# Who issues the quantiser's weight transfers inside attention: ScalarE, or SyncE at the end of its steps

## The reference, cut to what matters

```
h = layernorm(x) * (1 + ca) + sa
x = x + ga * attention(h)                      # rope, causal softmax, 4 query heads share a key/value head
h = layernorm(x) * (1 + cb) + sb
x = x + gb * ffn(h)

ternary_quant(w): w = bf16(w); in groups of 64:
    scale = max(mean(|w|), 1e-8);  q = clip(round(w / scale), -1, 1);  w + (q * scale - w)
ffn: gate, up = split(h @ quant(w_gate_up).T);  a = silu(gate) * up;  rms_norm(a) @ quant(w_proj).T
```

## Time and profile before

| | |
|---|---|
| time, median of 3 runs | 1734.54 us (1732.52 to 1736.47) |
| the profiled execution | 1730.82 us, span of its instructions 1729.0 us |
| TensorE busy | 1675.4 us (97%) |
| VectorE busy | 1248.8 us (72%) |
| ScalarE busy | 1140.5 us (66%) |
| GpSimd busy | 977.1 us (57%) |
| TensorE's granted clock, mean | 0.994 of full speed |
| SyncE's transfers (queue q1) | 140.99 MB, 28.7% of the 16 transfer engines' time |
| ScalarE's transfers (queue q10) | 48.25 MB, 10.2% |

### The profile page before, as it was taken

One profiled execution on the slowest core, in us unless ns is written; L12 is line 12 of the kernel. 1 busy time (PEld: TensorE's weight loads), 2 busy tenths in 40 slices (PEclk: granted clock), 3 DMA queues, 4 the chain that ended last, 5 costly groups with the idle time before them and its releaser, 6 DMA issues. The chain is left out here.

```text
span 1729.0 us, 27586 instructions
## 1 busy us (share of the span) xinstructions
PE 1675.4 (97%) x8993; PEld 1386.7 (80%) x8993; DVE 1248.8 (72%) x2518; ACT 1140.5 (66%) x2315; POOL 977.1 (57%) x822
## 2 busy tenths in 40 slices
PE   6899999999999999999999999889999899999998
PEld 2588888888888888888888888667788688888886
DVE  6788889888889888888888988873333564545433
ACT  4588888888888888888888888863232443323222
POOL 1367777777777777777677777445000245444453
PEclk9999999999999999999999999999999999999999
DMA  7234444445445354454354454456555101001000
GB/s 295 71 106 118 131 122 124 122 112 137 112 117 142 99 132 126 103 139 128 96 148 114 107 132 126 132 152 203 188 187 173 53 1 31 25 13 43 0 31 25
DMA packets 174969, 190.92 MB, mean 110 GB/s; under 512 B 31456, under 2 KB 117736, under 8 KB 174832
## 3 DMA queue, kind: packets, MB, share of 16 engines
q1 hardware_dynamic: 137840, 140.99, 28.7%
q10 hardware_dynamic: 36992, 48.25, 10.2%
HBM read 86.12 MB, written 31.74 MB: 68 GB/s over the span
## 5 line engine op out<-in xcount | busy, mean ns | idle before, releaser
L1102 DVE TENSOR_TENSOR p_lo<-ps_b,p_hi 128x512 fp32r<-128x512 f32 x576 | 395.1, 688 | 103.3 <-ACT p_hi L987 99.5
L987 ACT CAST p_hi<-ps_b 128x512 fp32r<-128x512 f32 x576 | 338.2, 589 | 116.3 <-PE ps_b L889 87.7
L1002 ACT ACTIVATE p<-ps_b,negm 128x640 f32<-128x640 f32 (+7 forms) x512 | 382.9, 752 | 41.2 <-DVE negm L1113 39.8
L1113 DVE CUSTOM_DVE_ANT_0 ps_b<-ps_b,mask_w 128x640 f32<-128x640 f32 (+7 forms) x512 | 385.4, 760 | 21.6 <-PE ps_b L878 17.6
L889 PE MATMUL ps_b<-ident,p 128*128 128x128 f32 x2304 | 345.6, 274 | 9.2 <-DVE p_lo L1102 9.1
L889 PEld LDWEIGHTS ps_b<-ident,p 128*128 128x128 f32 x2304 | 271.9, 140 | 56.1 <-DVE p_lo L1102 13.4
L877 PE MATMUL ps_b<-k_hh,q_hl 128*128 128x512 f32 (+3 forms) x768 | 265.6, 347 | 7.5 <-ACT p L1002 6.8
L903 PE MATMUL ps_b<-p_hi,v_hl 128*128 128x512 f32 x576 | 257.9, 448 | 4.0 <-ACT o_sb L995 3.5
L878 PE MATMUL ps_b<-k_l,q_hl 128*128 128x512 f32 (+3 forms) x768 | 256.2, 347 | 0.0
L904 PE MATMUL ps_b<-p_lo,v_hl 128*128 128x512 f32 x576 | 226.6, 393 | 0.0
L1741 PE MATMUL ps_d<-h_hi,gu 128*128 128x512 f32 x512 | 200.6, 392 | 2.4 <-DVE h_lo L1861 2.4
(11 more groups left out here) (160 smaller groups left out, 3123.6 us busy)
## 6 DMA issues: line engine op xcount, KB each, us to landing
rot_x<-rot_s SPq DMA_DIRECT2D x320, 64.0 KB, 2.0
q_hl<-rot_s SPq DMA_DIRECT2D x128, 128.0 KB, 2.6
q_hl<-rot_x SPq DMA_DIRECT2D x128, 128.0 KB, 2.8
rd_all<-reciprocals SPq DMA_DIRECT2D x128, 128.0 KB, 3.0
o_low<-o_sb ACTq DMA_DIRECT2D x128, 128.0 KB, 2.3
attention_out<-o_sb SPq DMA_DIRECT2D x128, 128.0 KB, 2.5
o_raw<-attention_out SPq DMA_DIRECT2D x32, 512.0 KB, 4.7
wf<-in_L_ffn_w_gate_up ACTq DMA_DIRECT2D x28, 256.0 KB, 3.1
```

The costliest lines, as they stand in the source:

```text
L987: act.copy(p_hi[:, T % P_RING, :], ps[:, T_BANK + T % 2, :]).then_inc(phi_ready, 1)
L1002: act.activation(p_32[:, parity, h, column * P:column * P + nk], s, ACT.Exp, bias=negm[:, k:k + 1], scale=-1.0, accum_out=den[:, parity, k ...
L1102: dve.tensor_tensor(p_lo[:, T % P_RING, :], ps[:, T_BANK + T % 2, :], p_hi[:, T % P_RING, :].bitcast(F32), ALU.subtract).then_inc(plo_read ...
L1113: dve.tensor_tensor_reduce(s, s, mask_w[:, S - nk:S], 1.0, HIGHEST, ALU.add, ALU.min, negm[:, k:k + 1]).then_inc(max_ready, 1)
```

## The change

The two kinds of transfer are issued by SyncE instead of ScalarE, in the same steps, at places 350 and 360, behind everything else that SyncE issues in a step. The functions take the engine as an argument and stand ahead of all engines' programs, so that the output projection can still call them for ScalarE. Waits and semaphores are the same.

```
-UNIT_STORES = Places(own_units(15), 620)
-UNIT_LOADS = Places(own_units(0), 630)
+UNIT_STORES = Places(own_units(15), 350)
+UNIT_LOADS = Places(own_units(0), 360)
...
+        def store_unit(eng, g, u):
+            to = unit_of(g, u, tern_gu_g, tern_p_g)
+            units_tern.await_(eng, g, u)
+            eng.dma_start(to, unit_tile(u, w_hat)).then_inc(tern_out, 16)
+
+        def unit_load(eng, g, u):
+            units_sign.await_(eng, g, u - 1)
+            eng.dma_start(unit_tile(u, unit_raw(g, u)), unit_of(g, u, gu_g, wp_g)).then_inc(wf_in, 16)
...
         # SyncE's step, behind the O_LOAD part and ahead of WEIGHT_LOADS in the text
+                for g, u in body.units(T, at, UNIT_STORES):
+                    store_unit(sp, g, u)
+                for g, u in body.units(T, at, UNIT_LOADS):
+                    unit_load(sp, g, u)
-            bodies(step, SWAPS, PLACINGS, SAVES, SPREADS, STORES, WEIGHT_LOADS)
+            bodies(step, SWAPS, PLACINGS, SAVES, SPREADS, STORES, WEIGHT_LOADS, UNIT_STORES, UNIT_LOADS)
...
         # ScalarE's step
-                for g, u in body.units(T, at, UNIT_STORES):
-                    store_unit(g, u)
-                for g, u in body.units(T, at, UNIT_LOADS):
-                    unit_load(g, u)
...
-            outputs.scalar(act, unit_load, unit_parts, store_unit)
+            outputs.scalar(act, lambda g, u: unit_load(act, g, u), unit_parts, lambda g, u: store_unit(act, g, u))
```

More of the change, by code:

```diff
@@ L717, in unit_tile, with unit_raw @@
             return tile[:] if u >= 2 else tile[:].rearrange("p (r h) -> p r h", r=2)
+        gu_g = w_gu.rearrange("(g u p) d -> g u p d", g=KVH, p=P)
+        wp_g = w_p.rearrange("(u r p) (g h) -> g u p r h", u=2, p=P, g=KVH)
+        tern_gu_g = tern_gu.rearrange("(g u p) d -> g u p d", g=KVH, p=P)
+        tern_p_g = tern_p.rearrange("(u r p) (g h) -> g u p r h", u=2, p=P, g=KVH)
+        def unit_raw(g, u):
+            return places.wf_late if g == KVH - 1 and u >= LAST_UNITS else wf
+        def store_unit(eng, g, u):
[5 more added lines that the diff above has]
+            eng.dma_start(unit_tile(u, unit_raw(g, u)), unit_of(g, u, gu_g, wp_g)).then_inc(wf_in, 16)
         def quarters(ap, kind):
@@ L952, in _ @@
         def _(act):
[L953 to L956, removed]
             def shift(g, n):
@@ L960, in shift @@
                 act.dma_start(o_low[:, n % 2, :], o_sb[D:P, n % 2, :]).then_inc(o_shifted[n % 2], 16)
[L962 to L972, removed]
             def unit_abs(g, u):
@@ L1082, in step @@
                     unit_sign(g, u)
-                for g, u in body.units(T, at, UNIT_STORES):
-                    store_unit(g, u)
-                for g, u in body.units(T, at, UNIT_LOADS):
-                    unit_load(g, u)
             bodies(step, KEY_SCALES, ROUNDINGS, VALUE_ROWS, VALUE_HIGHS, HIGHS, COPIES, SHIFTS, EXPONENTIALS, KEY_HIGHS, QUERY_HIGHS,
-                   UNIT_ABS, UNIT_SIGNS, UNIT_STORES, UNIT_LOADS)
+                   UNIT_ABS, UNIT_SIGNS)
             def unit_parts(g, u):
```

## The result

The changed kernel took 1750.80 us (median of 4 runs, 1749.59 to 1752.01) against 1733.53 us before in the same sessions: ratio 1.0099, 95% interval 1.0084 to 1.0115. It is slower by about 17 us, 2 us more than the 1748.5 that were predicted, and inside the range. A second session with the same kernel gave 1.0084 (1.0066 to 1.0103).

A forecast was written before the change was run, and what follows sets the result against it. TensorE was taken to bound seven of eight head groups, busy 937.4 of 940 us. Losses of 7 x (1.17 + 0.77) = 13.6 us take 1730.82 to 1744.5, or 1748.5 on the median; 8-in-10 range 1738 to 1759.

The forecast's parts named there:

- ScalarE's relief is worth nothing: Removing 88 issues, some 32 us, from ScalarE's queue gains between 0 and 2.6 us on the path, taken as 0.
- Four of the six units are early enough, and the stores too: Loads at SyncE's step end come early enough for four units; the tightest store keeps 2.2 us before VectorE's pick.
- Units 2 and 5 come 1.79 and 2.31 us ahead of Abs: Behind SyncE's other transfers, these loads start a mean 1.79 and 2.31 us before ScalarE's Abs, over seven groups.
- Landing 3.16 and 3.51 us, from the spreads at that place: Loads of units 2 and 5 take the mean times of SyncE's spreads issued there, 3.16 and 3.51 us.
- Waits of 1.37 and 1.20 us: ScalarE's Abs waits for its load 1.37 us at unit 2 and 1.20 us at unit 5, each once a group.
- The slack of TensorE, 0.2 and 0.43 us: Slack behind Abs: some 0.2 us at unit 2; at unit 5 0.19 us ScalarE idle plus 0.24 us before the scores.
- The place where it shows: TensorE loses 1.17 us behind unit 2's block copy and 0.77 us behind unit 5's exponential, idle at steps 28 and 63.
- The sum of 13.6 us: TensorE's loss over seven groups, 7 x (1.17 + 0.77) = 13.6 us, with the last group unchanged.
- The ring order: On SyncE's ring the load would queue behind the placing's transfers, landing nearer to 3.5 us; spreads and loads don't part this.

The follow-up runs named there:

- Both early: Changed kernel with SyncE's load of unit 2 at step 22 instead of 24, unit 5 at 57 instead of 60; 1734.54 us, ratio 1.0003.
- front of the step: Changed kernel with the loads at place 50 instead of 360 of the same steps on SyncE; 1737.50 us against 1734.57, ratio 1.0016.
- stores on ScalarE: Changed kernel with the stores moved back to ScalarE and the loads left on SyncE; 1748.18 us, ratio 1.0091.
- unit 5 early: Changed kernel with only the load of unit 5 moved, to step 57 instead of 60 on SyncE; 1741.63 us, ratio 1.0050.
- after again: The changed kernel run once more without further edits, for a second trace; ratio 1.0084.
- late on ScalarE: Kernel before, all unit transfers on ScalarE, with loads of units 2 and 5 issued late at steps 26 and 62; 1746.16 us, ratio 1.0067.

## Why the prediction was right, point by point

**ScalarE's relief is worth nothing**: right as far as the time can tell. Both early stands at 1.0003 (0.9992 to 1.0014) with all 88 issues moved. One reading was incomplete: of TensorE's waits from 80 to 1020 us before, one of 0.8 us ended on ScalarE's copy of a projection (rot_c), not on p_lo.

**Four of the six units are early enough, and the stores too**: right. No wait of Abs appears at units 1, 3 and 4, and none at unit 0 but the first; pick doesn't wait for a store in groups 0 to 6.

**Units 2 and 5 come 1.79 and 2.31 us ahead of Abs**: nearly at unit 2, low at unit 5. The time from the load's issue to Abs, less the wait, gives 3.43 - 1.57 = 1.86 us and 3.82 - 1.22 = 2.60 us. I spoke of a placing, a spread and a store in step 60; two of the three are of step 59. The reading of the time didn't depend on that, but the edit to the front of the step did.

**Landing 3.16 and 3.51 us, from the spreads at that place**: a little low. At unit 2 the first trace has 3.43 us, with one load of group 5 at 4.7, and its second trace, the kernel with the stores on ScalarE and the one with unit 5 early have 3.18 to 3.25. At unit 5 it is 3.69 to 4.01 us. The loads carry 256 KB and the spreads 128; I had named the size and not added for it, but no run shows that the size is the reason.

**Waits of 1.37 and 1.20 us**: 1.57 and 1.22 in the first trace, 1.35 and 1.34 in the second. At unit 5 of the first trace that is luck: the load was issued 0.29 us earlier before Abs than I had put, and landed 0.31 us later, and the two errors cancel. The single waits scatter more than the 1 to 1.5 us that I gave, from 0.83 to 2.70.

**The slack of TensorE, 0.2 and 0.43 us**: right. At unit 5 it can be read from six traces against the 311.03 us of both early: (8.55 - 5.80) / 7 = 0.39 after, (9.36 - 6.56) / 7 = 0.40 after again, (7.86 - 5.13) / 7 = 0.39, (10.07 - 7.38) / 7 = 0.38, (9.98 - 7.23) / 7 = 0.39, and late on ScalarE (4.22 - 1.55) / 7 = 0.38. In the kernel with the loads at the front of the step, waits of 0.21, 0.28 and 0.35 us left the spacing of their group at the 44.4 us that it has without any, and one of 0.84 us added 0.46. A cost that is the wait less a constant, over waits from 0.4 to 2.5 us, and nothing below it, is the mechanism as forecast. At unit 2 the spacing gives no such number: without a wait it lies anywhere from 345.0 to 348.4 us in these traces, and against 345.0 the same sum gives 0.20 (unit 5 early), 0.11 (stores on ScalarE), -0.12 (after again, and late on ScalarE) and -0.15 (after). TensorE's own records do give it. With no wait of Abs (before, and both early) the values start 0.27 to 0.35 us after the block copy has ended; in the changed kernel it is 0.05 us, but for one group of seven. So 0.22 to 0.30 us of it was slack. At unit 5 the scores start 0.27 us after the exponential in most groups before and 0.05 us after it in the changed kernel: 0.22 us, and with ScalarE's 0.19 us of idle time 0.41.

**The place where it shows**: right on what ends last, incomplete on what is hit first. I named the block copy at unit 2. TensorE stands before that at a projection, which waits for w_lo, that for w_hi, and that for Abs: seven waits of TensorE, 7.1 us. I had seen the rounding behind Abs on ScalarE and not followed who reads it. The copy is held as well and adds 0.1 us (from the projection to the values 0.89 us, 0.78 before). So it still sets the sum, which hardly changed. At unit 5 I named the exponential. The values are hit first there, by the copy, and the exponential adds 0.2 us (from the values to the scores 1.11 us, 0.90 before) and sets the sum.

**The sum of 13.6 us**: 14.5 and 14.7 us in the two pairs of traces. With the measured terms it is 7 x (1.57 - 0.25) + 5.8 = 15.0 us for the first trace and 7 x (1.35 - 0.25) + 6.6 = 14.3 us for the second. The medians say 17.3 and 13.2 us (14.6 by the ratio of the second session). The stretch behind group 6, which I had left unchanged, differs by 1.8 to 6.7 us in the pairs of traces, with the same work in it. The unchanged kernel's own runs spread over 1729 to 1739 us at mean granted clocks of 0.986 to 0.994. The clock of that stretch was lower in the changed kernel's first trace than in that of before, which is enough for 7 us, and as low in the fast kernel with both early. That makes it the executions' own with good reason; whether a small rest of it belongs to the change stays open.

**The ring order**: by the Trainium skill ("DMA: Bandwidth & Descriptors", "Queues, rings and completion order"), which has descriptors of one ring consumed in order, I had the load queue behind the placing. The late kernels show no such cost at unit 2 (3.43 and 3.24 us from SyncE, 3.62 from ScalarE) and at most 0.2 to 0.5 us at unit 5. What the Trainium skill says of the 16 engines that all issuers share (same page, "Issuing engines are not separate DMA queues") agrees better with unit 2. Neither is settled by these runs.

## What to carry to other kernels

A transfer that moves to another engine's list starts when that engine comes there in its own time: lay the two timelines side by side, and compare issue plus landing with the start of its reader. An engine that is idle for much of the time can still be behind just where it has a burst to issue. If the reader stands in the list of an engine that feeds a full one, each such wait beyond a few tenths of a us (here 0.2 to 0.3 and 0.4) is lost for good. Follow everything that stands behind the waiting instruction to its readers, not only the first one that comes to mind. Place the load by a step in which the issuer is waiting, and "early in the step" only means what it says for entries of that same step.

## What the runs showed of the hardware that was not expected

The same 256 KB load takes 0.33 to 0.37 us to issue on ScalarE. On SyncE its length goes by what stood ahead. Right behind transfers of 64 to 128 KB, whose own issues took about 0.6 us each, it took 0.58 to 0.62 us, now and then up to 0.86. Right behind the small saves of the denominators, of 0.3 us each, it took 0.36 us (unit 4 in the changed kernel, unit 5 in both early), and as much after 0.37 us of idle time. So part of an issue's length isn't the transfer's own; what it is, no run shows.

At both places the load stands behind a burst: a swap, a placing and a store at unit 2 (nine transfers), and a spread besides at unit 5 (ten). At unit 2 it landed no later than the late load from ScalarE, at unit 5 0.2 to 0.5 us later. With only the store taken away from ahead of it, in the kernel with the loads at the front of the step, it still landed 3.7 us after its issue at unit 5, so the number of transfers ahead doesn't explain the difference.
